# A chain of four blocks on one core: the first norm of the next block, its turns and its copies placed beside the feed-forward of this block

## What is computed

```python
# L2, after its self-attention
h = _layernorm(x, ln2_g, ln2_b)                      # the norm called n8 in the kernel
x = _attention(h, cond_emb, ca_wq, ca_wk, ca_wv, ca_wo, ca_bo) + x    # "cb"
h = _layernorm(x, ln3_g, ln3_b)                      # n9
p = h @ ff_w1 + ff_b1
a, gate = (p[..., :D_FF], p[..., D_FF:])
h = a * jax.nn.gelu(gate, approximate=False) @ ff_w2 + ff_b2
x = h + x                                            # "ff"
# L3
attn = softmax(where(mask, x Wq (c Wk)^T / sqrt(D), -inf))            # "cc"
out = (attn (c Wv)) Wo + x
out = (out - mean) * rsqrt(var + EPS) * gamma + beta                  # n10
```

## Time and profile before

| | us |
|---|---|
| median of 3 runs | 2163.55 |
| lowest, highest | 2161.96, 2166.22 |
| the profiled execution, its own time | 2163.22 |
| its span, first to last instruction | 2161.5 |
| the second chain inside it, about | 1745 to 2161 |

### The profile page before, as it was taken

How to read it: one execution, slowest core, us unless ns; L and a number is a source line. 1 busy time by engine, 2 the same in 40 slices (tenths; PEclk the granted TensorE clock), 3 DMA queues, 4 the chain that set the end, 5 groups by cost and what they waited for, 6 DMA issues and landing times. The chain is left out here.

```text
span 2161.5 us, 26638 instructions
## 1 busy us (share of the span) xinstructions
PE 2026.4 (94%) x10302; PEld 1203.4 (56%) x10302; DVE 1134.4 (52%) x2025; ACT 930.7 (43%) x1441; POOL 773.1 (36%) x563
## 2 busy tenths in 40 slices
PE   5999998898898999999999999999999999999997
PEld 3544444576676854444544454444543867676776
DVE  4677762535445357756555555555453243536353
ACT  3356666233433425555355544555456422222221
POOL 1222211122223126667566655665463010202121
PEclk9999999899999989999999999999999999999999
DMA  7724332000000020100000000000000510000000
GB/s 147 138 32 57 41 51 84 1 1 1 0 1 1 1 66 26 44 1 1 1 1 1 1 1 1 2 1 1 1 1 1 166 41 1 1 10 10 0 10 10
DMA packets 48044, 51.81 MB, mean 24 GB/s; under 512 B 14682, under 2 KB 38940, under 8 KB 47620
## 3 DMA queue, kind: packets, MB, share of 16 engines
q1 hardware_dynamic: 47924, 50.19, 11.3%
HBM read 41.24 MB, written 8.80 MB: 23 GB/s over the span
## 5 line engine op out<-in xcount | busy, mean ns | idle before, releaser
L1904 POOL TENSOR_TENSOR total<-total,pr 128x1024 f32<-128x1024 f32 x183 | 444.3, 2428 | 230.8 <-ACT pr L2114 214.0
L2114 ACT ACTIVATE pr<-sc 128x1024 f32<-128x1024 f32 x256 | 260.0, 1023 | 266.7 <-PE sc L1780 262.1
L1925 DVE TENSOR_REDUCE pmax<-ring 128x1 f32<-128x512 f32 x512 | 314.5, 683 | 98.2 <-PE ring L1728 98.2
L1780 PE MATMUL sc<-q_full,k_full 64*128 64x512 f32 x1024 | 295.0, 589 | 0.0
L1798 PE MATMUL o<-pr,v_pair 128*64 128x512 f32 x1024 | 247.7, 605 | 0.0
L1728 PE MATMUL ring<-k_round,q_round 64*128 64x512 f32 x512 | 214.1, 568 | 6.0 <-DVE k_round L1919 2.0
L645 ACT ACTIVATE probs<-s 128x512 f32<-128x512 f32 (+1 forms) x304 | 154.8, 579 | 95.4 <-PE s L360 94.6
L975 POOL TENSOR_TENSOR c_scores<-c_scores,c_total 128x1024 f32<-128x1024 f32 (+1 forms) x48 | 76.5, 1615 | 326.9 <-DVE c_total L924 326.9
L483 DVE TENSOR_REDUCE row_max<-s 128x1 f32<-128x1024 f32 (+3 forms) x128 | 125.1, 1019 | 58.2 <-PE s L346 57.8
L1728 PEld LDWEIGHTS ring<-k_round,q_round 64*128 64x128 f32 x512 | 78.4, 189 | 137.5 <-DVE pmax L1925 115.4
L1780 PEld LDWEIGHTS sc<-q_full,k_full 64*128 64x128 f32 x1024 | 129.0, 191 | 25.9 <-issue 16.8
(11 more groups left out here) (342 smaller groups left out, 3438.8 us busy)
## 6 DMA issues: line engine op xcount, KB each, us to landing
qk_dram<-qk_parts SPq DMA_DIRECT2D x32, 192.0 KB, 2.7
q_stack<-qk_dram SPq DMA_DIRECT2D x48, 128.0 KB
k_stack<-qk_dram SPq DMA_DIRECT2D x48, 128.0 KB
x<-in_x SPq DMA_DIRECT2D x4, 512.0 KB, 7.4
region<-in_L_xattn_mlp_w SPq DMA_DIRECT2D x2, 1024.0 KB, 7.8
region<-in_L_xattn_ff_w SPq DMA_DIRECT2D x1, 2048.0 KB, 18.6
out<-region SPq DMA_DIRECT2D x8, 256.0 KB, 2.2
region<-in_L_xattn_sa_wo SPq DMA_DIRECT2D x1, 1024.0 KB, 7.7
```

The lines of the kernel that those rows point to most:

```text
L1780: ins = te.matmul(s2[at % 2][:, j], kf[n % 2][head[j], keys], qf[n % 2][head[j], halves[half]], start=False, stop=True)
L1904: pool.tensor_tensor(out=total[half][:], in0=other[:], in1=probs[at % KEPT][:], op=ALU.add).then_inc(sums, 1)
L1925: dve.tensor_reduce(part_max[:, j, t, half:half + 1], ring[bank_of_max(i)][:], AX.X, ALU.max).then_inc(s1_free, 1)
L2114: act.activation(probs[here % KEPT][:], s2[at % 2][:], ACT.Exp).then_inc(s2_free, 1)
```

## The change

In words, in five parts, all between one block and the next:

- VectorE computes n8 of block i + 1 between the last gated product of the feed-forward of block i and the addition `xc`; it stood after the last PSUM copy of cc and ahead of `x.last`. It has statistics, moments and `rstd` of its own (class `Ahead`).
- GpSimd's two steps of each stream stand ahead of its four multiplications of cc; they stood behind them.
- TensorE turns n8 of a stream directly behind the turn of that stream's `xc`, in the scores of cc; it did so after the values of cc.
- ScalarE copies the turned n8 of a stream directly behind that stream's `x.T`; it did so after the last exponential of cc.
- TensorE waited for `x.last` of both streams ahead of the first matmul of the next block's scores. Now it waits for stream 0's there, and for stream 1's after the first score tile.

The steps of n8 count on three semaphores of their own, one per engine and shared by both streams; the first n8, made in the stage before, has its five semaphores merged into two, and an unused one is gone.

```diff
-def scores_tensor(te, ch, e, name, i, lhs, lhs_ready, m, cols, bias, turn, rows_later=None):
+def scores_tensor(te, ch, e, name, i, lhs, lhs_ready, m, cols, bias, turn, rows_later=None, ahead=None):
...
-        after(te, ch.act[s], lhs_ready, i)
+        if ahead is None:
+            after(te, ch.act[s], lhs_ready, i)
+        else:
+            after(te, ahead.act, f"{lhs_ready}{s}", i)
...
@@ part_chain2, tensor @@
                 def turn_x(s):
                     after(te, ch.dve[s], "xc", i)
                     turn_tensor(te, ch, e, ch.xc[s], s, 0).then_inc(ch.te[s].sem, ch.te[s].one("x.T"))
+                    if not last:
+                        turn_ahead(i + 1, s)
+
+                def turn_ahead(i, s):
+                    after(te, ahead.dve, f"n8.h{s}", i)
+                    turn_tensor(te, ch, e, ch.h[s], s, 3).then_inc(ahead.te.sem, ahead.te.one(f"n8.T{s}"))
...
                 if not last:
-
-                    for s in range(B):
-                        turn_step(te, ch, e, i + 1, "n8", s, 3)
-                    for s in range(B):
-                        after(te, tail.dve[s], "x.last", i)
-                    head(i + 1)
+                    head(i + 1, lambda s: after(te, tail.dve[s], "x.last", i))
@@ vector @@
             def head(i):
-                for s in range(B):
-                    norm_vector(dve, ch, "n8", i, lambda s: tokens(e, s, i), streams=[s])
+                one = lambda n, s: (ahead.dve.sem, ahead.dve.one(f"n8.{n}{s}"))
+                for s in range(B):
+                    for t in range(2):
+                        ins = dve.bn_stats(ahead.stats[s][:, t, :], tokens(e, s, i)[:, t, :])
+                    ins.then_inc(*one("stats", s))
...
+                if not last:
+                    head(i + 1)
                 for s in range(B):
                     add_vector(dve, ch, e, "xc", i, "ff.down", s, ch.xc[s][:])
                 cross_vector(dve, ch, "cc", i, 512)
-                if not last:
-                    head(i + 1)
@@ scalar @@
                 for s in range(B):
                     after(act, ch.te[s], "x.T", i)
                     turned_scalar(act, ch, s, 0, ch.xT[s]).then_inc(*one(s, "x.T"))
+                    if not last:
+                        head(i + 1, s)
                 cross_scalar(act, ch, "cc", i, 512)
-                if not last:
-                    head(i + 1)
```

More of the change, by code:

```diff
@@ L698, in __init__ @@
         self.power = ch.power
+class Ahead:
+    def __init__(self, nc, ctx, ch, name):
+        sem = lambda n: ctx.enter_context(nc.semaphore(n))
+        steps = lambda engine, names: Steps(sem(f"{name}_ahead_{engine}"), [f"{n}{s}" for s in range(B) for n in names])
+        self.te, self.act = steps("tensor", [f"{name}.T"]), steps("scalar", [f"{name}.hT"])
+        self.dve = steps("vector", norm_steps(name))
+        self.pool = steps("gpsimd", [f"{name}.shifted", f"{name}.rstd"])
+        self.made = ch.sb("made", [1, 5])
+        self.stats, self.moments, self.rstd, self.spare = (
+            ch.sb(f"{name}_{n}", shape) for n, shape in (("stats", [P, 2, 6]), ("moments", [P, 2, 2]), ("rstd", [P, 2]),
+                                                         ("spare", [1, 1])))
 def chain_blocks(engine, emit):
@@ L2202, in _ @@
                                pattern=[[64, 2]], channel_multiplier=-1).then_inc(gp.sem, gp.one("second"))
[L2203 to L2205 removed]
+            pool.memset(n8_power[:], -0.5).then_inc(n8_gpsimd.sem, n8_gpsimd.one("power"))
+            pool.wait_ge(n8_gpsimd.sem, n8_gpsimd.value("power"))
+            pool.wait_ge(n8_vector.sem, n8_vector.value("moments"))
             pool.tensor_tensor(out=n8_rstd[:], in0=n8_moments[:, :, 1], in1=e.eps[:].to_broadcast([P, 4]),
[L2207 to L2209 removed]
+                               op=ALU.add).then_inc(n8_gpsimd.sem, n8_gpsimd.one("shifted"))
+            pool.wait_ge(n8_gpsimd.sem, n8_gpsimd.value("shifted"))
+            pool.tensor_tensor(out=n8_rstd[:], in0=n8_rstd[:], in1=n8_power[:], op=ALU.pow).then_inc(n8_gpsimd.sem, n8_gpsimd.one("rstd"))
         @block.vector
@@ L2398, in part_chain2 @@
         gate, inner = e.gate, ch.pT
-        made = ch.sb("made", [1, 5])
-        result = e.result
+        result, made = e.result, ahead.made
         stored = [ctx.enter_context(nc.semaphore(f"out_stored{s}")) for s in range(B)]
@@ L2419, in _, with head @@
         def _(te):
-            def head(i):
-                scores_tensor(te, ch, e, "cb", i, ch.hT, "n8.hT", e.m2, 1024, None, lambda s: None)
+            def head(i, free):
+                scores_tensor(te, ch, e, "cb", i, ch.hT, "n8.hT", e.m2, 1024, None, free, ahead=ahead)
             def emit(i, first, last):
@@ L2477, in head @@
             def head(i):
+                one = lambda n, s: (ahead.dve.sem, ahead.dve.one(f"n8.{n}{s}"))
                 for s in range(B):
-                    norm_vector(dve, ch, "n8", i, lambda s: tokens(e, s, i), streams=[s])
+                    for t in range(2):
+                        ins = dve.bn_stats(ahead.stats[s][:, t, :], tokens(e, s, i)[:, t, :])
+                    ins.then_inc(*one("stats", s))
+                    after(dve, ahead.dve, f"n8.stats{s}", i)
+                    dve.memset(ahead.spare[s][:], 0.0)
+                    for t in range(2):
+                        ins = dve.bn_aggr(ahead.moments[s][:, t, :], ahead.stats[s][:, t, :])
+                    ins.then_inc(*one("moments", s))
+                    after(dve, ahead.pool, f"n8.rstd{s}", i)
+                    for t in range(2):
+                        ins = dve.tensor_scalar(ch.h[s][:, t, :], tokens(e, s, i)[:, t, :], ahead.moments[s][:, t, 0:1],
+                                                ahead.rstd[s][:, t:t + 1], ALU.subtract, ALU.mult)
+                    ins.then_inc(*one("h", s))
             def finish_block(i, waits):
@@ L2496, in emit @@
                         for k, name in enumerate(norm_steps("n8")):
-                            dve.memset(made[s][:, k:k + 1], 0.0).then_inc(*one(s, name))
+                            dve.memset(made[s][:, k:k + 1], 0.0).then_inc(ahead.dve.sem, ahead.dve.one(f"{name}{s}"))
                     mask_rows(dve, ch, e.biases2, 2 * C)
@@ L2531, in _, with head @@
             one = lambda s, name: (ch.act[s].sem, ch.act[s].one(name))
-            def head(i):
-                for s in range(B):
-                    after(act, ch.te[s], "n8.T", i)
-                    turned_scalar(act, ch, s, 3, ch.hT[s], w.vec["ln2_g"], w.vec["ln2_b"]).then_inc(*one(s, "n8.hT"))
+            def head(i, s):
+                after(act, ahead.te, f"n8.T{s}", i)
+                turned_scalar(act, ch, s, 3, ch.hT[s], w.vec["ln2_g"], w.vec["ln2_b"]).then_inc(
+                    ahead.act.sem, ahead.act.one(f"n8.hT{s}"))
             def emit(i, first, last):
                 if first:
-                    head(0)
+                    for s in range(B):
+                        head(0, s)
                 cross_scalar(act, ch, "cb", i, 1024)
@@ L2570, in emit @@
                         for k, name in enumerate(("n8.shifted", "n8.rstd")):
-                            pool.memset(made[s][:, 3 + k:4 + k], 0.0).then_inc(ch.pool[s].sem, ch.pool[s].one(name))
+                            pool.memset(made[s][:, 3 + k:4 + k], 0.0).then_inc(ahead.pool.sem, ahead.pool.one(f"{name}{s}"))
                 cross_gpsimd(pool, ch, "cb", i, 1024)
@@ L2575, in emit @@
                     norm_gpsimd(pool, tail, e, "n10", i - 1)
+                if not last:
+                    for s in range(B):
+                        after(pool, ahead.dve, f"n8.moments{s}", i + 1)
+                        pool.tensor_tensor(out=ahead.rstd[s][:], in0=ahead.moments[s][:, :, 1],
+                                           in1=e.eps[:].to_broadcast([P, 2]), op=ALU.add).then_inc(
+                            ahead.pool.sem, ahead.pool.one(f"n8.shifted{s}"))
+                        after(pool, ahead.pool, f"n8.shifted{s}", i + 1)
+                        pool.tensor_tensor(out=ahead.rstd[s][:], in0=ahead.rstd[s][:], in1=ch.power[:],
+                                           op=ALU.pow).then_inc(ahead.pool.sem, ahead.pool.one(f"n8.rstd{s}"))
                 cross_gpsimd(pool, ch, "cc", i, 512)
-                if not last:
-                    norm_gpsimd(pool, ch, e, "n8", i + 1)
-                else:
+                if last:
                     norm_gpsimd(pool, tail, e, "n10", i)
```

26 lines of the change are left out of this document (13 added, 13 removed).

## The result

| | before | changed |
|---|---|---|
| median, us | 2164.06 (4 runs) | 2147.93 (4 runs) |
| lowest to highest | 2161.96 to 2166.22 | 2147.55 to 2148.86 |
| the profiled execution's span | 2161.5 | 2147.1 |

The ratio is 0.9931, with a 95% interval of 0.9920 to 0.9943: faster by 12 to 17 us. The prediction was 2149.2 (2146.5 to 2153.5). Its sum of 14.34 us is close to what was gained, and the runs cannot tell it from the truth; the traces can, since the scatter of this kernel lies ahead of the changed stage.

The account below looks back on a forecast made before the run. TensorE, busy 94% of the span, was taken to bound the kernel. Net boundary gains of 4.71, 4.83 and 4.80 sum to 14.34 us, other terms 0: 2163.55 - 14.34 = 2149.2 us, range 2146.5 to 2153.5.

Parts of the forecast that it names:

- Part 1: Block boundary, from cc's last values to VectorE's first maximum: 8.88 us becomes 3.64, removing 5.24, 5.15 and 5.27.
- part 5: New waits and register instructions on TensorE: cost 0, at the other end 0.8 us; a gain there excluded.
- The clock's share in the tiles: Four score tiles at the boundary: 15.00 us instead of 13.92, so 1.08 us for half clock.
- Its share in the turn: Stream 1's turn at the boundary: 1.12 us instead of 0.60, so 0.52 us for half clock.
- Part 2: n8 turns in cc's scores: stream 0's costs 0, stream 1's 0.44 us; net 4.71, 4.83 and 4.80 per boundary.
- Part 3: ScalarE's copies of n8 in cc: cost 0, hidden with -0.05 us of room; at worst 0.58 per block.
- Part 4: Both norms, 5.44 us on VectorE, moved ahead of `xc`: 10.1 us available, cover 4.7 more than needed.
- rival 1: In cc, ScalarE's copy becomes the path: up to 0.58 us a block, 1.7 in all, 2150.9; chance 0.08.
- rival 3: Boundary: release not per stream, or TensorE meets stream 1's `x.last` before the first tile: 2.3 to 3.1 us; chance 0.03.
- The clock in cc (2): In cc the clock falls: 1.6 us in each of three blocks, 4.8 in all, 2154.0; chance 0.04.
- The slow side (4): Norms on VectorE hold `xc`: gain gone at 14.9 us of norms, 2168 at 16.3 us; chance 0.02.
- Nothing was given back within cb (5): In cb the gain is given back, and the time stays near 2163 us; chance 0.03.

Follow-up runs that it names:

- second: The changed kernel measured again, nothing altered, beside the kernel before: median 2147.72 us over 5 runs, ratio 0.9932, 14.6 us less.
- release of both: Changed kernel, but TensorE again waits for `x.last` of both streams ahead of the first score product: 2150.97 us (before 2162.82).

## Why the prediction was right, and where its steps were off

**Part 1, the boundary.** From the start of the scores to the first maximum I had 3.64 us; it is 2043.99 - 2040.36 = 3.63. What failed is where the scores start. I put them where the turn had stood, 3.71 us behind the start of the last values (2049.45 - 2045.74). They start 3.46 behind it (2040.36 - 2036.90). That turn had itself waited: in the trace of before its first weight load starts 0.05 us after VectorE has written stream 0's n8 (2048.66 + 0.74 = 2049.40), with a bracket that the matmul's row does not have.

```profile
2048.66 0.74 DVE L743 TENSOR_SCALAR vcol<-x,c_moments,c_rstd 128x256 f32 x2 [1.09 <-POOL c_rstd L755]
2049.45 0.42 PEld L815 LDWEIGHTS c_ps<-ident,vcol 128*128 128x128 f32 x4 [0.50 <-DVE vcol L743]
```

So part 1 was wrong to say that TensorE begins whatever comes next at the end of cc's values, and the step of part 5 that said a gain in the starts behind waits "is excluded" was wrong in sign: 0.25 a boundary, 0.75 in all, which is nearly all of 15.2 - 14.34. The clock's share in the tiles, 1.08, is confirmed by the filling with transposes (3.2 us in three boundaries). Its share in the turn was put 0.06 too high: the prediction compared 1.12 with 0.60, but a turn that starts behind a wait takes 0.66 at full clock too (the same run), so the clock cost 0.46 there and 1.5 in all. The removed idle time and turns show in the version with only the norm moved.

**Part 2, the turns.** Stream 0's in the idle time, 0; stream 1's 0.44. From the turn of `xc` to the last values it was 2045.74 - 2029.44 = 16.30 and is 2036.90 - 2020.17 = 16.73: 0.43. Right: the wait of 0.72 us further on in cc did not absorb it, and the later turn, placed in that wait, gave it back.

**Part 3, ScalarE.** Cost 0 was right, the margin was not: 0.05 us of room worked out, 0.16 measured. The mis-sized term is the copy, 1.02 us. That is the length of its row, not what it adds to the queue: in the timeline of cc above, the copy of `x.T` starts at 2024.20, lasts 0.66, and the next copy starts at 2024.74, 0.12 before it ends. The first exponential, counted from the start of `x.T`, moved from 1.97 us (2035.44 - 2033.47) to 2.88 (2027.08 - 2024.20), by 0.91. With 0.91 in place of 1.02 the prediction's own sum gives the 0.16. The row of before that this uses:

```profile
2033.47 0.66 ACT L830 ACTIVATE c_xT<-c_ps 128x256 f32<-128x256 f32 x2 [2.73 <-PE c_ps L815]
```

**Part 4, VectorE.** 4.7 us of cover; `xc` of stream 0 ends at 2015.49 and is turned at 2020.17, which leaves 4.68. With 4.01 us more nothing moved, and with 7.93 us more TensorE waited.

**The sum against the time.** First set of runs 16.1 us, second 14.6, chain 15.2. The 0.9 us by which the first lies above the chain is of the size by which the start of the chain scatters; why the stages ahead of it scatter was not looked into. That the forecast of 2149.2 lies 1.3 us from the median is in part luck: the sum was 0.9 too small, and the scatter is of that size. The high end of the range was added up too low by its own terms: 2149.2 with rival 1 (1.7), the low price of rival 3 (2.3) and the 0.8 of part 5 is 2154.0 without any scatter, not 2153.5.

**The rivals.** The clock in cc (2) did not fall. TensorE did not meet stream 1's `x.last` (3); its price was put at 2.3 to 3.1 and the run that undoes the release shows 3.5. The slow side (4) begins where VectorE has 8 us more to do, and not at 14.9 - 5.44 = 9.5 us more: the prediction left out that the wait for `xc` brings a fall of the clock, 1.7 to 2.5 us a block. Nothing was given back within cb (5): the second maximum follows the first by 3.44 us as before.

## What to carry to other kernels

Price an idle time by what runs behind it too: here 2.11 us of waiting carried another 1.5 us of half clock, and useless transposes in the gap recovered about two thirds of that by themselves. When work is moved off a boundary, look for the next wait there at once, since the release per stream was worth 0.7 us before the norm went and 3.5 after it. And put moved TensorE work into a bracketed idle time rather than between products: the same turn cost 0.43 us in one place and nothing in another.

## What the runs showed of the hardware

An idle of 0.97 us (release of both) left the clock at 1.00; idle times of 2.11 us (before) and 3.06 us (VectorE 8 us longer) were followed by half clock, each time. The fall shows either as soon as TensorE works again or some time later, and the distance varies. In the run with the release alone, the same idle of 2.11 us stands at all three boundaries:

```profile
1844.98 1.12 PE L815 MATMUL c_ps<-ident,o_w 128*128 128x128 f32 x4 [2.11 <-DVE o_w L743]
1845.89 15.16 PE L846 MATMUL c_ps<-m,c_hT 128*128 128x512 f32 x32
...
1947.09 0.86 PE L815 MATMUL c_ps<-ident,o_w 128*128 128x128 f32 x4 [2.11 <-DVE o_w L743]
1947.77 15.49 PE L846 MATMUL c_ps<-m,c_hT 128*128 128x512 f32 x32
...
2049.31 0.69 PE L815 MATMUL c_ps<-ident,o_w 128*128 128x128 f32 x4 [2.11 <-DVE o_w L743]
2049.99 15.59 PE L846 MATMUL c_ps<-m,c_hT 128*128 128x512 f32 x32
```

The turn pays less each time and the scores more. The granted clock agrees: 0.50 from 1845 to 1846, 0.70 from 1947 to 1948, and 0.90 from 2049 to 2050 with 0.50 behind it. The two rows add up to 16.28, 16.35 and 16.28 us, so here it changes which instruction is slow, and the cost in all hardly changes.

That is not so everywhere. With 3.06 us of idle time the fall came at once in block 0 (the turn took 1.12) and cost 2.5 us; in blocks 1 and 2 the turn was fast (0.65 and 0.66), in block 2 the stage up to 2034.0, 1.5 us after TensorE had resumed, still has a granted clock of 1.00, and the fall cost 1.7. What sets the distance, no run here shows.
